# Two layers in one kernel: the experts' inputs gathered by one-hot products for four groups, and through DRAM for the other twelve

## The reference

```
x  = x + ga * mamba(modulated layer norm of x)
h2 = modulated layer norm of x
logits = h2 @ gate_w.T;  w, sel = top_k(softmax(logits), 8);  w = w / sum(w)
pos  = how many tokens before this one chose the same expert
slot = pos if pos < 64, else dropped
xin[expert, slot] = h2[token]                         # 64 experts x 64 rows x 256
out = (silu(xin @ wg) * (xin @ wu)) @ wd              # per expert, 96 hidden
x  = x + gb * sum over the 8 choices of w * out[expert, slot]
x  = x + ... windowed attention ...;   x = x + ... MLP with decoded 4-bit weights ...
```

## Time and profile before

| | us |
|---|---|
| three timed runs | 698.09, 701.3, 700.17; median 700.17 |
| profiled execution, its span | 697.7 |
| PE / DVE / ACT / POOL busy | 605.5 / 485.9 / 307.0 / 193.2 |
| state loop, about | 77 to 171 |
| expert stage, first table to the last store | 173.8 to 307.3 |

### The profile page before, as it was taken

The page is one execution under the profiler, slowest core; times in us unless marked ns, Lnnn a source line. Parts: engine busy times, 40 slices in busy tenths (PEclk is TensorE's granted clock), DMA queues, the critical chain, the costliest instruction groups (busy, mean ns, idle before and its releaser), DMA issues.

```text
span 697.7 us, 10429 instructions
## 1 busy us (share of the span) xinstructions
PE 605.5 (87%) x3540; PEld 472.3 (68%) x3540; DVE 485.9 (70%) x1046; ACT 307.0 (44%) x951; POOL 193.2 (28%) x240
## 2 busy tenths in 40 slices
PE   2999899974897999866569999999999899989995
PEld 0554577753876888544447776776777688878885
DVE  5847666653599899613797999999687556654444
ACT  1763356532132233222487887887886211111110
POOL 1226601101010001037754554340112265600000
PEclk9999999995899899867689999999999999999999
DMA  8200161100073799963211413320000000000000
GB/s 311 81 1 0 35 198 37 39 1 1 1 212 116 227 292 270 320 210 95 69 53 31 62 32 51 41 31 1 1 2 0 1 1 1 2 28 3 1 1 30
DMA packets 23364, 50.36 MB, mean 72 GB/s; under 512 B 5520, under 2 KB 8720, under 8 KB 22800
## 3 DMA queue, kind: packets, MB, share of 16 engines
q1 hardware_dynamic: 18960, 37.10, 17.2%
q0 software_dynamic: 4352, 12.59, 7.7%
HBM read 44.43 MB, written 5.24 MB: 71 GB/s over the span
## 4 chain that ended last, share of the span: by engine, by line
PE 51%; DVE 31%; issue 5%; ACT 5%; DMA 4%; SPq 3%; another core or an unknown queue 0%; DVEq 0%; ACTq 0%
PE bank L1286 48%; DVE spot L1034 3%; DMA arena<-in_w 2%; ACT arena L739 2%; DVE arena L1212 2%; DVE arena L1116 1%; SPq L315 1%; ACT arena L764 1%; DMA arena<-in_wmod 1%; DVE arena L1124 1%; DMA arena<-in_dsc 1%; DVE arena L936 1%; DVE arena L1054 1%; DVE arena L1055 1%; DVE arena L1053 1%
## 5 line engine op out<-in xcount | busy, mean ns | idle before, releaser
L1286 PE MATMUL bank<-arena 128*128 128x128 f32 (+9 forms) x1848 | 355.1, 377 | 32.3 <-DMA arena<-in_wmod 8.3
L1286 PEld LDWEIGHTS bank<-arena 128*128 128x128 f32 (+4 forms) x1848 | 241.6, 182 | 114.4 <-issue 73.1
L1286 PE MATMUL bank<-spot,h_hi 128*128 128x256 f32 x256 | 67.1, 300 | 9.5 <-DVE spot L1034 9.4
L846 ACT ACTIVATE arena<-bank 128x512 f32<-128x512 f32 x32 | 19.2, 599 | 113.4 <-PE bank L1286 113.4
L1286 PE MATMUL bank<-spot,h 128*128 128x256 f32 x256 | 65.3, 293 | 0.0
L1286 PEld LDWEIGHTS bank<-spot,h_hi 128*128 128x128 f32 x256 | 51.6, 202 | 15.3 <-DVE spot L1034 10.8
L1267 DVE TENSOR_TENSOR arena<-arena,bank 128x512 f32<-128x512 f32 x32 | 22.0, 687 | 56.6 <-ACT arena L846 56.6
L1286 PEld LDWEIGHTS bank<-spot,h 128*128 128x128 f32 x256 | 51.5, 201 | 0.0
L1286 PE MATMUL bank<-h_hi,low 128*128 128x512 f32 x128 | 50.1, 391 | 0.0
L576 ACT ACTIVATE arena<-bank,arena 128x256 f32<-128x256 f32 x32 | 16.3, 560 | 68.9 <-PE bank L1286 68.9
L1286 PE MATMUL bank<-h_hi,gu_hi 128*128 128x512 f32 x112 | 44.4, 397 | 1.0 <-issue 0.5
(11 more groups left out here) (244 smaller groups left out, 1103.9 us busy)
## 6 DMA issues: line engine op xcount, KB each, us to landing
arena<-in_wgu SPq DMA_DIRECT2D x32, 384.0 KB, 4.4
arena<-in_wd SPq DMA_DIRECT2D x32, 192.0 KB, 5.5
expert_out<-arena POOLq DMA_DIRECT2D x16, 256.0 KB, 5.4
arena<-in_w SPq DMA_DIRECT2D x1, 2048.0 KB, 10.4
arena<-in_wmod SPq DMA_DIRECT2D x1, 1536.0 KB, 14.8
arena<-in_w_in SPq DMA_DIRECT2D x1, 1288.0 KB, 8.8
arena<-in_x SPq DMA_DIRECT2D x1, 1024.0 KB, 5.6
arena<-in_wmod SPq DMA_DIRECT2D x1, 1024.0 KB, 11.8
```

The source lines that it names most:

```text
L846: act.activation(gl[n % 3], bank[2 * (n % 3)][:, :], ACT.Gelu_apprx_tanh).then_inc(gl_ready, 1)
L1286: return pe.matmul(o, lhsT, rhs, start=start, stop=stop, **kw)
```

## The change

The rows of the first four groups (`BY_TABLE = 4`) are made as before. For the other twelve groups the rows go through a new DRAM tensor `expert_in` (`xex`). POOL clears a part of SBUF early, SP writes zeros from it to all of `expert_in`, and the loads of the experts' weights wait for that. In the state loop DVE turns the slots of each tile into row numbers (`scatter8`, one more instruction in `place_rows`), and POOL issues eight indirect transfers per tile, 64 in all, that write rows of h2 to their places. The halves of h2 that POOL made are now made by DVE (`halves`, two instructions per tile, ahead of `less_maximum`), the rest in a place of its own, `h_lo`. In the expert stage SP issues `load_rows(g + 3)` first thing in its step g, 256 KB for group g+3, into one of three buffers; the first of them waits for all 64 scatters. PE transposes the loaded rows with four transposes. The tables of groups 4 to 15 are left out. The helper for products is gone (its calls are written out), and the arena is cut up otherwise.

```diff
+        h_lo = [at(A0 + 10496 + DM * t if t < 7 else XB + 768, DM) for t in range(T)]
+        spot = [at(A0 + 6400 + 2048 * i, T, 2 * P) for i in range(2)]
+        zeros = at(X0 + 2048, 2048)
+        scatter8 = at(A0 + 27440, T, TOPK).bitcast(u32)
+        BY_TABLE = 4
+        xg_s = [at(o, 2, DM) for o in (XB + 6144, A0 + 28368, A0 + 6400)]
         negpos = at(XB, T, E)
...
+            sp.wait_ge(zeros_ready, 1)
+            sp.dma_start(xex.rearrange("(p a b) c -> p a (b c)", p=P, b=8), zeros.unsqueeze(1).to_broadcast([P, 4, 2048])).then_inc(xex_zeroed, 16)
...
+            def load_rows(g):
+
+                i = (g - BY_TABLE) % 3
+                if g == BY_TABLE:
+                    sp.wait_ge(scattered, 16 * T * TOPK)
+                sp.wait_ge(xgT_mm, g - 2)
+                sp.dma_start(xg_s[i], xex[4 * CAP * g:4 * CAP * (g + 1), :].rearrange("(q p) c -> p q c", p=P)).then_inc(xg_loaded[i], 16)
...
+            sp.wait_ge(xex_zeroed, 16)
             for q, tile, early in ((0, 1, True), (1, 2, True), (2, 2, True), (3, 3, True), (6, 3, True), (4, 1, False),
                                    (5, 2, False), (7, 4, False), (8, 5, False)):
                 sp.wait_ge(st_mm if early else yT_mm, tile)
...
             for g in range(NG):
+                if BY_TABLE <= g + 3 < NG:
+                    load_rows(g + 3)
                 while n < NQ and n <= g - 1:
                     load_codes(n)
                     n += 1
...
+            pool.memset(zeros, 0.0).then_inc(zeros_ready, 1)
...
+            pool.wait_ge(xex_zeroed, 16)
             for t in range(T):
-                pool.wait_ge(rowsT_mm, T + t + 1)
-                if t >= 4:
-                    pool.wait_ge(st_mm, 4)
-                pool.tensor_copy(rounded(h_hi[t]), h[:, t, :]).then_inc(pool_chain, 1)
-                pool.wait_ge(pool_chain, T + t + 1)
-                pool.tensor_tensor(rounded(h[:, t, :]), h[:, t, :], rounded(h_hi[t]), ALU.subtract).then_inc(halves_ready, 1)
+                pool.wait_ge(h2_ready, t + 1)
+                pool.wait_ge(slots_ready, t + 1)
+                for k in range(TOPK):
+                    pool.indirect_dma_start(xex, bass.IndirectOffsetOnAxis(scatter8[:, t, k:k + 1], 0), h[:, t, :], None,
+                                            bounds_check=SLOTS - 1, oob_is_err=False).then_inc(scattered, 16)
 
...
-                dve.max(slot8[:, t, :], slotv[:, t, :])
+                link(dve.max(slot8[:, t, :], slotv[:, t, :]))
+                dve.tensor_scalar(scatter8[:, t, :], slot8[:, t, :], -1.0, NOWHERE, ALU.mult, ALU.add).then_inc(slots_ready, 1)
+
+            def halves(t):
+
+                dve.wait_ge(h2_ready, t + 1)
+                if t >= 4:
+                    dve.wait_ge(st_mm, 4)
+                link(dve.tensor_copy(rounded(h_hi[t]), h[:, t, :]))
+                dve.tensor_tensor(rounded(h_lo[t]), h[:, t, :], rounded(h_hi[t]), ALU.subtract).then_inc(halves_ready, 1)
 
...
+                    halves(s - 2)
                     less_maximum(s - 2)
...
-                if g + 2 < NG:
+                if g + 2 < BY_TABLE:
                     spots(g + 2)
...
             def rows_T(g):
-                pe.wait_ge(spot_ready, g + 1)
                 if g >= 2:
                     pe.wait_ge(xgT_ready, 2 * (g - 1))
+                if g >= BY_TABLE:
+                    i = (g - BY_TABLE) % 3
+                    pe.wait_ge(xg_loaded[i], 16 * ((g - BY_TABLE) // 3 + 1))
+                    for j in range(KC):
+                        for q in range(2):
+                            ins = pe.transpose(bank[g % 2][:, P * (2 * j + q):P * (2 * j + q + 1)], xg_s[i][:, q, j * P:(j + 1) * P], ident)
+                    ins.then_inc(xgT_mm, 1)
+                    return
+                pe.wait_ge(spot_ready, g + 1)
                 for j in range(KC):
                     for t in range(T):
-                        for part in (h_hi[t], h[:, t, :]):
-                            ins = mm(bank[g % 2][:, 2 * P * j:2 * P * (j + 1)], rounded(part[:, j * P:(j + 1) * P]), rounded(spot[g % 2][:, t, :]),
+                        for part in (h_hi[t], h_lo[t]):
+                            ins = pe.matmul(bank[g % 2][:, 2 * P * j:2 * P * (j + 1)], rounded(part[:, j * P:(j + 1) * P]), rounded(spot[g % 2][:, t, :]),
                                      start=t == 0 and part is h_hi[t], stop=t == T - 1 and part is not h_hi[t])
                 ins.then_inc(xgT_mm, 1)
```

More of the change, by code:

```diff
@@ L29, in adaln_two_layers @@
     yex = nc.dram_tensor("expert_out", (SLOTS, DM), f32, kind="Internal").ap()
+    xex = nc.dram_tensor("expert_in", (SLOTS, DM), f32, kind="Internal").ap()
     ctx = ExitStack()
@@ L173, in adaln_two_layers @@
             sem, ["h2_ready", "logits_mm", "lmax_ready", "exp_ready"])
-        mask_ready, pos_mm, place_read, halves_ready, spot_ready = map(
-            sem, ["mask_ready", "pos_mm", "place_read", "halves_ready", "spot_ready"])
+        mask_ready, pos_mm, place_read, halves_ready, spot_ready, slots_ready, scattered = map(
+            sem, ["mask_ready", "pos_mm", "place_read", "halves_ready", "spot_ready", "slots_ready", "scattered"])
+        zeros_ready, xex_zeroed = sem("zeros_ready"), sem("xex_zeroed")
+        xg_loaded = [sem(f"xg_loaded{i}") for i in range(3)]
         wout_ready, cols_mm = sem("wout_ready"), sem("cols_mm")
@@ L245, in adaln_two_layers @@
         X1 = X0 + 2048
-        places = [(2048, "h"), (4096, None)] + [(A0 + 2048 * i, "gu_hi") for i in range(4)] + [
-            (A0 + 7168, "spot"), (A0 + 9216, "spot"), (A0 + 11264, None)] + [(B0 + 2048 * i, "low") for i in range(6)] + [
+        places = [(A0 + 2048 * i, "gu_hi") for i in range(3)] + [
+            (A0 + 6144, "spot"), (A0 + 8448, "spot"), (A0 + 10496, "h_rest"), (A0 + 12288, "low")] + [
+            (B0 + 2048 + 1024 * i, "low") for i in range(10)] + [
             (D0, None), (D0 + 1536, "it_low"), (D0 + 3072, "it_hi"), (D0 + 4608, None), (A1, "h4_hi"),
@@ L1298, in project @@
                 for j in range(KC):
-                    ins = mm(o[:, 0:hi - lo], uT[:, j, t * P:(t + 1) * P], w_in_s[:, j, lo:hi], start=j == 0, stop=j == KC - 1)
+                    ins = pe.matmul(o[:, 0:hi - lo], uT[:, j, t * P:(t + 1) * P], w_in_s[:, j, lo:hi], start=j == 0, stop=j == KC - 1)
                 ins.then_inc(done, 1)
@@ L1400, in _ @@
                             pe.wait_ge(yo_ready, s - 1)
-                        mm(bank[4][:, :], cT[:, s, :], state[:, s % 2, :]).then_inc(Yo_mm, 1)
+                        pe.matmul(bank[4][:, :], cT[:, s, :], state[:, s % 2, :]).then_inc(Yo_mm, 1)
                 if 0 <= s - 2:
@@ L1413, in _ @@
                     pe.wait_ge(xD_ready, s + 1)
-                    mm(bank[3][:, :], ident, xD[s], start=True, stop=False, skip_group_check=True)
+                    pe.matmul(bank[3][:, :], ident, xD[s], start=True, stop=False, skip_group_check=True)
                 if 0 <= s - 1 < T:
@@ L1436, in _ @@
                     for j in range(4):
-                        ins = mm(bank[7][:, 0:DM], yT[:, t % 2, j * P:(j + 1) * P], w_out_s[:, j, :], start=j == 0, stop=j == 3)
+                        ins = pe.matmul(bank[7][:, 0:DM], yT[:, t % 2, j * P:(j + 1) * P], w_out_s[:, j, :], start=j == 0, stop=j == 3)
                     ins.then_inc(o_mm, 1)
@@ L1619, in scores_a @@
                 for i, o in enumerate((bank[0], bank[1])):
-                    mm(o[:, :], ident_b, mask_first_b if t == 0 else mask_win_b, start=True, stop=False, skip_group_check=True)
+                    pe.matmul(o[:, :], ident_b, mask_first_b if t == 0 else mask_win_b, start=True, stop=False, skip_group_check=True)
                     for j in range(4):
                         p = 4 * i + j
-                        ins = mm(o[:, j * P:(j + 1) * P], qT[:, 0, 2 * p:2 * p + 2, :].rearrange("p a b -> p (a b)"), keys,
+                        ins = pe.matmul(o[:, j * P:(j + 1) * P], qT[:, 0, 2 * p:2 * p + 2, :].rearrange("p a b -> p (a b)"), keys,
                                  start=False, stop=True, skip_group_check=True)
@@ L1693, in project_out_a @@
                 for i in range(0, 5):
-                    mm(bank[4][:, 0:DM], aT[t % 2][:, i, :], w12_s[:, i, :], start=i == 0, stop=i == NH - 1, skip_group_check=True)
+                    pe.matmul(bank[4][:, 0:DM], aT[t % 2][:, i, :], w12_s[:, i, :], start=i == 0, stop=i == NH - 1, skip_group_check=True)
             def project_out_b(t):
@@ L1802, in _ @@
                         for k, (l, r) in enumerate(((hi, xhi), (hi, xlo), (lo, xhi))):
-                            ins = mm(bank[2 * (n % 3) + a][:, :], rounded(l), rounded(r), start=j == 0 and k == 0,
+                            ins = pe.matmul(bank[2 * (n % 3) + a][:, :], rounded(l), rounded(r), start=j == 0 and k == 0,
                                      stop=j == 1 and k == 2)
```

62 lines of the change are left out of this document (29 added, 33 removed).

## The result

The changed kernel takes 735.28 us (median of four runs, 735.16 to 737.71), the kernel before in the same runs 699.13: ratio 1.0532, 95% interval 1.0497 to 1.0567. It is slower by 36 us, and 734 was forecast. The first lines are those of the page's head, of a group on PE and of the scatters, and of the rows' loads (busy, mean ns; idle before and for whom; then KB and median us to landing).

A forecast was written before the change was run, and what follows sets the result against it. It saw PE and DVE in turn bounding the state loop, and PE, DVE, DMA and SP nearly tied in the expert stage. 697.7 + 5.0 state loop + 28.5 ring + 2.5 span to median gave 734 us, range 714 to 750.

The forecast's parts named there:

- State loop: `halves` and `scatter8` on DVE add 4.7 us to the state loop, taken as 5 us, bounds 0 and 8.3.
- Scatters: POOL's 64 scatters end at 198, about when SP asks for rows: a wash, 2 us of wait PE does not see.
- scatters late: Rival, chance 0.06: scatters take as long as the longest gather, end at 242, and the total is 776 us.
- The ring: Expert stage: rows, PE, decode, codes and SP's next rows wait in a circle, 20.8 us per two groups; chance 0.62.
- The clock: After long waits in the expert stage PE runs at half clock, so its 2.8 us per ring become 5.6.
- Where the ring starts: From group 5's rows, issued at 201.99, decode ends at 218.2 and group 7's rows go at 224.2, without the state loop's 5.
- The end: Behind the last rows stands the same work as before, 14.4 us to the last store.
- SP alone sets the pace, and the cut work pays: Rival, chance 0.08: codes do not wait, a step is SP's 6.4 us; 693 us, or 698 with the state loop's 5.

The follow-up runs named there:

- e2: The kernel before with the state-loop change alone (DVE's `halves` and `scatter8`, no POOL halves, no scatters): 704.83 us, ratio 1.0063.
- e1: The changed kernel with SP asking for the rows one step earlier, group g+4 instead of g+3 in step g: 704.34 us, ratio 1.0065.
- e11: The changed kernel with only DVE's order changed: pieces decoded one group earlier, routing weights one per group behind, pieces reordered: 701.77 us, ratio 1.0045.
- e4: The changed kernel with the scales of a piece of codes in one transfer instead of eight (two for the last four pieces): 734.09 us, ratio 1.0498.
- e5: e4 with only a quarter of the columns of each expert pair that SP loads in the expert stage: 711.28 us, ratio 1.0198.
- e7: e1 with `halves` right behind `normed` in the state loop, then the top 8 and `scatter8`: 696.83 us, ratio 0.9979.
- e9: e8 with pieces decoded one group earlier on DVE, routing weights one per group behind, pieces in another order: 690.31 us, ratio 0.9893.
- e10: e9 with the scales of a piece in one transfer (two for the pieces of down): 695.89 us, ratio 0.9959.
- e8: e7 with the first two pieces of codes issued ahead of the rows of group 4: 697.91 us, ratio 0.9999.

## Why the prediction was right

- **State loop**, 5 us: 5.8 (179.57 against 173.75), 0.91 per round instead of 0.8. e2 has it alone. In the runs with this same state loop the first table starts anywhere from 177.8 to 181.9, so the round is the surer number.
- **Scatters**, a wash: 1.034 us and a gap of 0.30 each, ended at 195.67 where 198 was said; SP asked for the rows at 200.98 and never waited for them. The rival "scatters late" is out. All but the first of the 15 scatters that took 1.1 us or more began while DVE was in a product of two operands in SBUF, and each ended 0.85 us after that product; the 15 together lost 3.9 us. The Trainium skill, page "SBUF — State Buffer", section "SBUF: two separate sides", says that a DVE operation with two SBUF inputs and a GpSimd operation that reads SBUF shut each other out, whichever starts first: the trace agrees, though the price is small here. No scatter of this run began during one of the copies of `halves`, which the prediction had in mind.
- **The ring**, 20.8 us: 20.35 on average over four turns, and for the reason given; e1 and e11 open it at two places and lose most of the 36 us. Its terms were less exact than their sum: landing 5.0 to 5.8 instead of 4.6, SP 6.0 to 6.2 instead of 5.96, and PE 4.1 to 4.3 instead of 5.6, since the four transposes took 1.09 and the others 0.43 and 2.6 to 2.8. That the landing grows with the bytes ahead of it (e4 against e5) I had not had as a term.
- **The clock.** In the last 3 us of each of PE's waits of 8 to 15 us the granted clock was 0.50, and `gate_up` behind them took 2.6 to 2.8 us instead of 1.5, as said; in the even groups from 8 on, after waits of 0.9 to 2.0 us, twice 2.8 and twice 1.5.
- **Where the ring starts.** The first turn's decode was to end at 223.2, with the state loop's 5: it ended at 228.8. This is the term that was furthest off. The rows of group 5 were issued at 208.29 (207.0 said) and landed after 7.2 us (4.6), and PE's work up to the end of `gate_up` behind them was at half clock already, 4.3 us (2.8): 1.3, 2.6 and 1.5 of the 5.6 us.
- **The end.** From the last rows ready (323.6) to the last store 11.1 us instead of 14.4. This and the 1.8 us saved by the rings took back nearly all of the late start. That 734 was met to 1.3 us is in part luck; that the ring was forecast, and what closes it, is not.
- **SP alone sets the pace, and the cut work pays.** Rejected for the kernel as it is, but e7 to e9 show where it leads: once the decoder hardly holds SP up, SP issues without a pause and the DMA engines are full (e9, 690.31, where the rival named 693 for a state loop that costs nothing). Which of the two then sets the pace is not shown; e10 takes work from SP, but has a price of its own. I had no term for the 256 KB that each group adds; at the 284 GB/s of e1 they are 0.9 us per group.

## What to carry to other kernels

A queue that issues transfers for two consumers ties them together: a load that must come early should not stand behind one that waits for late work. What to check is whether one turn of the circle fits into the groups that it spans: 20.35 us are 10.2 per group over two groups and 6.8 over three, where a group took 6.5 before. Cutting work from PE and DVE won nothing as long as the DMA engines were as full as in e1; there, look for bytes that can move to an idle stretch (e8), and for the wait that keeps them from it (e9). Where an engine stands idle in every round, as DVE here for 1.6 us, added work was free in that place (e7) and cost nearly its full length a few instructions away (0.91 of 1.04 us).

## What the runs showed of the hardware

An indirect write of 128 rows of 1 KB cost POOL 1.03 us on average and 0.30 us between two, less than the indirect reads' 1.07 to 1.16; 49 of the 64 took less than 1.0, and the 14 that began 0.26 to 0.65 us before the end of a DVE product of two SBUF operands ended 0.85 us after that end. The DMA engines gave 284 GB/s (e1) to 296 (e9) on this mix at a share of 1.06, and 320 at 1.01 in another stretch of e9, so a share near 1 does not stand for one rate. The same 256 KB of scales in one transfer of 8 rows, each copied to 16 partitions, made e10 5.6 us slower than e9 with its eight transfers of 32 KB, although SP had half as much to issue; in the changed kernel (e4) it made no difference.
